# Attention scores read by the exponent with the row minimum as bias, normalisations moved from VectorE to ScalarE, and the written-out orders redone

## What is computed

```
x = x + tanh(g_xattn[0]) * xattn0(layernorm(x), ctx, mask)     # "A": 4 heads of 64, one shared K/V head, rotary, 120 context rows, masked
x = x + tanh(g_ffn[0])   * ffn0(layernorm(x))                  # "F": 256 -> 704 -> 256, SiLU gate, inputs and hidden rounded blockwise to FP4
x = x + tanh(g_xattn[1]) * xattn1(layernorm(x), ctx, ctx)      # "B": 16 heads of 16, 120 context rows
x = x + tanh(g_ffn[1])   * moe(layernorm(x))                   # "R": router, best 2 of 8 experts; then the experts, 256 -> 1024 -> 256
```

## Time and profile before

| | |
|---|---|
| time before | 1921.44 us, median of 3 runs (1916.14 to 1923.22) |
| the profiled execution | 1920.27 us, its span 1918.6 us |
| first stage, preparation | 0 to about 200 us |
| first stage, 15 steps between L1101's first and last | 201.1 to 1191.2 us |
| experts' stage | about 1306 to 1919 us |
| PE, DVE, ACT, POOL busy | 1572.6, 1236.2, 738.9, 643.7 us |

### The profile page before, as it was taken

The page is one execution under the profiler, slowest core; times in us unless marked ns, Lnnn a source line. Parts: engine busy times, 40 slices in busy tenths (PEclk is TensorE's granted clock), DMA queues, the critical chain, the costliest instruction groups (busy, mean ns, idle before and its releaser), DMA issues.

```text
span 1918.6 us, 36797 instructions
## 1 busy us (share of the span) xinstructions
PE 1572.6 (82%) x12221; PEld 1252.5 (65%) x12222; DVE 1236.2 (64%) x3068; ACT 738.9 (39%) x1545; POOL 643.7 (34%) x624
## 2 busy tenths in 40 slices
...
DMA packets 63099, 123.78 MB, mean 65 GB/s; under 512 B 13890, under 2 KB 51899, under 8 KB 58811
## 3 DMA queue, kind: packets, MB, share of 16 engines
...
## 4 chain that ended last, share of the span: by engine, by line
PE 73%; DVE 13%; issue 6%; ACT 4%; DMA 2%; POOL 2%; SPq 0%; DVEq 0%; ACTq 0%; POOLq 0%
PE bank L1243 17%; PE bank L1245 16%; PE bank L1244 16%; PE bank L1315 7%; PE bank L1339 6%; PE bank L1328 4%; PE bank L1407 1%; ACT b_q L736 1%; PE bank L1463 1%; PE bank L1517 1%; DVE b_sx L1008 1%; DVE b_mx L1006 1%; DVE b_rv L926 1%; PE bank L1427 1%; ACT b_pt L684 1%
## 5 line engine op out<-in xcount | busy, mean ns | idle before, releaser
L1243 PE MATMUL bank<-split_room,wm 128*128 128x256 f16 x1152 | 314.7, 273 | 8.5 <-issue 6.9
L1245 PE MATMUL bank<-split_room,wm 128*128 128x256 f16 x1152 | 314.6, 273 | 0.0
L1244 PE MATMUL bank<-split_room,wm 128*128 128x256 f16 x1152 | 314.6, 273 | 0.0
L1220 DVE SCALAR_TENSOR_TENSOR split_room<-bank,b12e,split_room 128x256 f32<-128x256 f32 x288 | 138.1, 483 | 265.1 <-ACT split_room L786 260.1
L786 ACT ACTIVATE split_room<-bank,b12e 128x256 f32<-128x256 f32 x288 | 134.5, 471 | 195.3 <-PE bank L1245 191.3
L1315 PE MATMUL bank<-b_k,b_q 128*128 128x480 f32 x256 | 139.5, 629 | 34.7 <-ACT b_q L736 28.7
L647 POOL DMA_INDIRECT acc<-split_room,m_cur x72 | 115.3, 1602 | 131.7 <-ACT split_room L800 105.9
L1243 PE MATMUL bank<-wm,split_room 128*128 128x256 f16 x576 | 157.0, 273 | 0.0
L1244 PE MATMUL bank<-wm,split_room 128*128 128x256 f16 x576 | 157.0, 273 | 0.0
L1245 PE MATMUL bank<-wm,split_room 128*128 128x256 f16 x576 | 157.0, 273 | 0.0
L1339 PEld LDWEIGHTS bank<-b_v,b_pt 120*128 120x128 f32 x1024 | 132.9, 199 | 36.8 <-issue 30.5
(11 more groups left out here) (352 smaller groups left out, 3984.2 us busy)
## 6 DMA issues: line engine op xcount, KB each, us to landing
...
```

The costliest lines, as they stand in the source:

```text
L1220: dve.scalar_tensor_tensor(m_h[:, c % 3], bank[c % 4][:, TILE:2 * TILE], b12e[:, p, 1, c:c + 1], m_s[:, c % 2], ALU.add, ALU.mult).then_in ...
L1243: pe.matmul(o, lh, rh, start=start, stop=False)
L1244: pe.matmul(o, ll, rh, start=False, stop=False)
L1245: return pe.matmul(o, lh, rl, start=False, stop=stop)
```

## The change

It has five parts.

1. The scores are computed with their sign turned (the scale of the queries is negative, the mask's fill too), so that `exp(s - max s)` is `exp(-n + min n)`. DVE takes the minimum of each row alone; ACT reads the scores in PSUM with scale -1 and the minimum as a bias, which needs an instruction for each of the 4 heads. The subtraction and its tile are gone, and PE waits for `G.exp` instead of `G.sub` before it writes the next scores.
2. The four normalisations and the scaling of the context go from DVE to ACT as `x * rs + nb`, with `nb = -mean * rs`; POOL computes `nb` with two more instructions in `pow_`.
3. In R.rank the gate is folded into the reciprocal: two DVE instructions fewer.
4. `ORDER` is written anew for all five engines. The weight stages (`W`) stand two or three steps earlier, and the loop runs over steps 4 to 13 instead of 3 to 14.
5. Two bias tiles of the preparation share memory with `b_ex`.

```diff
-            "POOL": ("B.ln/2 W2/3 R.ln/3 A.ln/-1 F.p0/1 F.p1/1 F.ln/0 R.scatter/3 F.p/0 W0/2 W1/2").split(),
+            "POOL": ("A.ln/-1 W0/0 W1/0 F.p0/1 F.p1/1 R.scatter/3 F.ln/0 W2/0 F.p/0 B.ln/1 R.ln/2").split(),
...
-        FIRST_LOOP, END_LOOP, STEPS = 3, 15, NB + max(LAGS)
+        FIRST_LOOP, END_LOOP, STEPS = 4, 14, NB + max(LAGS)
...
-            def pow_(G, rv, rs, n):
+            def pow_(G, st, rv, rs, nb, n):
+
                 def stage(b, p):
                     pool.wait_ge(G.stats, b + 1)
-                    pool.tensor_tensor(rs[:, 0:n], rv[:, 0:n], mhalf[:, 0:n], ALU.pow).then_inc(G.rsqrt, 1)
+                    if not isinstance(b, int) or b >= 1:
+                        pool.wait_ge(A.c if G is A else G.z, b)
+                    pool.tensor_tensor(nb[:, 0], st[:, 0:NT, 6], mone[:, 0:NT], ALU.mult)
+                    pool.tensor_tensor(rs[:, 0:n], rv[:, 0:n], mhalf[:, 0:n], ALU.pow).then_inc(G.power, 1)
+                    pool.wait_ge(G.power, b + 1)
+                    pool.tensor_tensor(nb[:, 1], nb[:, 0], rs[:, 0:NT], ALU.mult).then_inc(G.rsqrt, 1)
                 return stage
...
+            def normalise(G, x_t, rs, nb, z):
+                def stage(b, p):
+                    held(act, G.rsqrt, b + 1)
+                    if G is R:
+                        held(act, R.free, b + 2)
+                    for t in range(NT):
+                        last = act.activation(z[:, t], x_t[:, p, t], ACT.Identity, bias=nb[:, 1, t:t + 1], scale=rs[:, t:t + 1])
+                    last.then_inc(G.z, 1)
+                    if G is A:
+                        act.activation(a_c, ct[:, p], ACT.Copy, scale=a_rs[0:S, 2:3]).then_inc(A.c, 1)
+                return stage
...
                     def stage(b, p):
-                        held(act, G.sub, b * n + k + 1)
-                        act.activation(ex[:, k % 2], sx[:, k % 2], ACT.Exp).then_inc(G.exp, 1)
+                        held(act, G.mn, b * n + k + 1)
+                        for h in range(QUAD):
+                            last = act.activation(ex[:, k % 2, h], sb_[:, h * S:(h + 1) * S], ACT.Exp,
+                                                  bias=mn[:, k % 2, h:h + 1], scale=-1.0)
+                        last.then_inc(G.exp, 1)
...
                         s4 = sbk[:, 0:QUAD * S].rearrange("p (h s) -> p h s", h=QUAD)
-                        dve.tensor_reduce(mx[:, k % 2], s4, AX.X, ALU.max).then_inc(G.mx, 1)
-                        dve.wait_ge(G.mx, b * n + k + 1)
-                        dve.tensor_tensor(sx[:, k % 2], s4, over(mx[:, k % 2], S), ALU.subtract).then_inc(G.sub, 1)
+                        dve.tensor_reduce(mn[:, k % 2], s4, AX.X, ALU.min).then_inc(G.mn, 1)
...
-                    for t in range(NT):
-                        last = dve.tensor_scalar(G.zs[:, t], G.x[:, p, t], G.st[:, t, 6:7], G.rs[:, t:t + 1], ALU.subtract, ALU.mult)
-                    last.then_inc(G.z, 1)
...
-                cr.link(dve.tensor_scalar(r_w[:, 0], r_e[:, :], 1.0, None, ALU.add))
-                cr.wait()
-                cr.link(dve.reciprocal(r_w[:, 0], r_w[:, 0]))
+                cr.link(dve.tensor_scalar(r_w[:, :], r_e[:, :], 1.0, g_inv[:, 0:1], ALU.add, ALU.mult))
                 cr.wait()
                 held(dve, R.pair_free, b + 1)
                 pw = r_pair[:, p].bitcast(f32)
-                dve.tensor_scalar(pw[:, 0, :, 1], r_w[:, 0], gate[:, 3:4], None, ALU.mult)
-                cr.link(dve.tensor_tensor(r_w[:, 1], r_w[:, 0], r_e[:, :], ALU.mult))
+                cr.link(dve.reciprocal(pw[:, 0, :, 1], r_w[:, :]))
...
                         else:
-                            pe.wait_ge(G.sub, b * n + k)
+                            pe.wait_ge(G.exp, b * n + k)
```

More of the change, by code:

```diff
@@ L352, in gated_stack @@
         ORDER = {
-            "SP": ("A.load/-1 W/2 B.out/3 B.load/0 R.rank/3").split(),
-            "POOL": ("B.ln/2 W2/3 R.ln/3 A.ln/-1 F.p0/1 F.p1/1 F.ln/0 R.scatter/3 F.p/0 W0/2 W1/2").split(),
-            "ACT": ("B.t0/3 B.s2/3 B.t1/3 B.t2/3 B.s3/3 F.ht1/2 A.s0/0 B.t3/3 B.s4/3 B.s5/3 A.s1/0 A.t0/0 B.t4/3 B.s6/3 "
-                "B.t5/3 A.t1/0 B.s7/3 B.t6/3 B.t7/3 F.t/1 B.ot/3 F.gu0/1 A.ot/0 F.gu1/1 B.ct/2 B.zt/2 F.gu2/1 R.t/3 "
-                "R.logit/3 F.gu3/1 B.k/2 B.q/2 A.t/-1 B.s0/2 B.s1/2 F.ht0/1").split(),
[3 rows of a table removed]
-                "F.q0c/1 B.s0/2 A.t/-1 B.v/2 B.s1/2 F.q1b/1 B.s2/2 F.q1c/1").split(),
[3 rows of a table removed]
-                "F.gu3/1 B.k/2 B.q/2 B.s0/2 A.t/-1 B.v/2 B.s1/2 A.kv/-1 F.ht0/1 B.t0/2 B.s2/2 A.q/-1").split(),
+            "SP": ("A.load/-1 B.load/1 W/0 B.out/3 R.rank/3").split(),
+            "POOL": ("A.ln/-1 W0/0 W1/0 F.p0/1 F.p1/1 R.scatter/3 F.ln/0 W2/0 F.p/0 B.ln/1 R.ln/2").split(),
+            "ACT": ("B.k/3 B.q/3 B.s0/3 B.s1/3 B.t0/3 F.ht0/2 B.s2/3 B.t1/3 B.t2/3 B.s3/3 A.s0/0 F.ht1/2 B.t3/3 B.s4/3 B.s5/3 "
+                "B.t4/3 F.z/1 A.s1/0 A.t0/0 B.s6/3 A.t1/0 B.t5/3 B.s7/3 B.t6/3 B.t7/3 F.t/1 B.ot/3 A.ot/0 F.gu0/1 B.z/2 "
+                "F.gu1/1 R.z/3 R.t/3 B.ct/2 B.zt/2 F.gu2/1 A.z/-1 A.t/-1 R.logit/3 F.gu3/1").split(),
[3 rows of a table added]
+                "F.q0c/1 B.s0/2 F.q1b/1 F.q1c/1").split(),
[3 rows of a table added]
+                "R.rank/3 B.k/2 B.q/2 A.kv/-1 B.s0/2 A.q/-1 B.v/2 B.s1/2 B.t0/2 F.ht0/1 B.s2/2 B.p0/2").split(),
         }
         LAGS = [int(entry.split("/")[1]) for order in ORDER.values() for entry in order]
-        FIRST_LOOP, END_LOOP, STEPS = 3, 15, NB + max(LAGS)
+        FIRST_LOOP, END_LOOP, STEPS = 4, 14, NB + max(LAGS)
         def step(order, stages, s, odd, static):
```

113 lines of the change are left out of this document (57 added, 56 removed), and 12 rows, old and new, of the table ORDER.

## The result

The changed kernel takes 1943.6 us (median of three executions, 1941.9 to 1944.8; a fourth of 4932 us was slow and is left out) against 1918.8 for the kernel before on the same chip: ratio 1.013, 95% interval 1.009 to 1.017. The forecast was 1845 us; the change makes the kernel 1.3% slower. The profiled execution has a span of 1940.3 us.

The account below looks back on a forecast made before the run. PE's waits were taken to decide the first stage: 4.3 us less idle and 1.1 less low clock make 5.4 a step, times 14 is 76, so 1921.4 - 76 = 1845 us; range 1790 to 1922 (8 in 10).

Parts of the forecast that it names:

- transposes: PE's wait at the second transposes for ACT's copy, now behind four exponents: 0.9 us a step becomes 1.3.
- r_z: New PE wait for R's normalised operand, as R.t lost F.gu2 as cover: 4.7 us against 3.8 covered, 0.9.
- b_q: PE's wait at B's first scores for ACT's queries: 1.8 us a step, A.kv covers 0.95, 0.5 counted.
- exponents: New PE waits a step for ACT's exponents: B.s1 behind the table load, 0.45 us; B.s2 with little cover, 0.8.
- the 1.1 that was set for small waits: PE's idle time a step outside the six listed waits, taken as 1.1 us as before.
- clock (1.1): Low PE clock in the first stage costs 3 us a step; 0 to 3 comes back, 1.1 taken.
- So 14 steps count: 14 x 5.4: First stage: 14 steps each gain 5.4 us (4.3 idle, 1.1 clock), 76 us in all.
- Ranks ... gone: PE's 1.85 us a step wait for DVE's one-hot chain vanishes, covered by A.t and F.gu3 (2.5 us).
- The splits rival: POOL's W0 and W1 slow R.logit and R.rank on DVE; gain falls by 3.2 to 2.2 us a step: 1890 us; chance 0.20.
- Edges ... 0: Start and end of the stage: 2 us each, set against each other; last two steps 0; no net effect.
- the case "slower": Rival: PE's scores wait for ACT's exponents ten times a step; at 0.9 us a round, 1971 us; chance 0.14.
- the forecast's own terms: Per step, low clock 0 to 3 us and idle 4.4 to 7 us, said to give 1810 to 1875 us.

Follow-up runs that it names:

- unrolled_w_later: Changed kernel with the hardware loop written out on every engine and POOL's first two weight splits moved behind the scatter: 1872.6 us, ratio 0.974.
- before_unrolled: Kernel before the change with its twelve loop steps written out: 1903.6 us, ratio 0.992.
- w_later: Changed kernel with POOL's first two weight splits moved from ahead of the dequantisation to behind the scatter: 1913.9 us, ratio 0.997.
- exponents_only: Kernel before with only the exponents and the pair weights changed, old orders and loop bounds, normalisations on DVE: 1963.1 us, ratio 1.019.

## Why the prediction was wrong

The forecast's sum, held against unrolled_w_later, which is the change without its two losses: forecast 61.3 us a step, measured 61.6. The waits, forecast and measured a step: transposes 1.3 and 1.35; r_z 0.9 and 1.2; b_q 0.5 and 0.9; exponents 1.25 and 0.8; B.ot 0.3 and 0.4. Not in the sum: b_v, 1.2, partly against the 1.1 that was set for small waits (the rows leave 17.1 / 13 = 1.3). An exponent takes 0.37 us (0.35) and a round's four 1.12 (1.1), a normalisation's instruction 0.59 by itself with two done in 1.08 (0.85), POOL's chain 1.13 (1.15). DVE has 41.8 us a step (41), ACT 36.4 (37). The clock in the steps is 0.96 for 0.93.

That 61.3 and 61.6 lie so close is in part luck. The 66.7 us from which the forecast took its 5.4 held the old kernel's own edges, and no term of the sum removes them; unrolled_w_later has none. Like against like, from the second to the thirteenth step: before 66.8 us (PE idle 9.5), before_unrolled 65.6 (8.7), unrolled_w_later 61.6 (5.4). The change without its losses gives 4.0 us a step, not 5.4: 3.3 of idle time (forecast 4.3) and 0.7 of clock (1.1). And its first step has 64.3 us where before_unrolled's has 55.3. So against before_unrolled it gains 31 us, not 76.

What failed:

1. **"So 14 steps count: 14 x 5.4".** The steps were taken as alike. I never asked where the new lists put the branch, though the loop stands in the code and the earlier trace rows give only the mean of 15 steps. In the kernel before the loop cost 20 us in all; in the changed one 45, of which the 20 were in the forecast's base. No rival foresaw it. The Trainium skill (Runtime: NRT & Kernel Launch, Instruction fetch mechanics) says that a taken branch out of the window of instructions forces a fetch before the engine goes on, and the runs agree: 1.4 to 4.2 us of stall on PE, 2.0 to 4.1 on DVE, none like it with the loop written out.
2. **"Ranks ... gone".** The sum gave the chain its old length, and it has 5.5 us instead of 1.4. The splits rival had the mechanism and its price right at 3.2 us a step (3.0 by w_later's steps), 26 to 30 us in the medians; its chance of 0.20 was too low, as the row of B.z at four times its time was in front of me. The Trainium skill (SBUF — State Buffer, SBUF: two separate sides) puts an exclusive lock between POOL's operations and those of DVE that have two SBUF inputs or run in a two-port mode. The runs agree for the forms with two inputs (161 to 1705 ns for r_d, the queries' sum 0.68 to 1.44 us, but 0.68 kept where one input is a bank). The router's cast, with one input, is hit as well (175 to 660 ns); the page would put that down to its mode, which no run here separates. The rule would have told that r_d and r_m are hit, where I wrote that I didn't know which forms are.
3. **"Edges ... 0".** From first to last: the first F.done is 3.0 us later in the changed kernel (9.3 in unrolled_w_later), the last F.done to the last pairs 3.9 longer (90.2 against 86.3 us), the rest to the end 6.5 (647.6 against 641.1). POOL's first read of the experts' ids waits for the final write of split weights in both kernels, and that write took 18.7 us to land for 17.2 before; this is 1.5 of the 6.5, and the rest was not looked for.

Together, in the spans: 40 us of edges (998.4 for 958.2 with the loop written out), where the kernel before has 23 (990.1 for 966.8), so 17 more; the steps apart from the edges 9 less (958.2 for 966.8); the ends 13.4 more. That makes the 21.7 us between the two spans. The range ended at 1922 and the case "slower" had 0.14, all of it for an exponents' bound that did not come: PE's scores wait 0.55 us a step for b_ex. That rival did exist, in the old orders: exponents_only has just this wait, and loses 39 us. The bounds of the forecast's own terms give 1805 to 1884 us when added up, not 1810 to 1875; neither holds the result.

What remains open: whether a better place exists for A.z on DVE, why the first F.done moves by 7 us with where DVE's list begins, the longer first step, and 5 us behind the last pairs.
